# A two-layer mixture-of-experts kernel: sixteen subtractions move from VectorE to GpSimd, and layer 1's dispatch scatters are held to two in flight

## The chip, the cores and the metric

The kernel runs on one core of a Trainium2 chip. The metric is device time in microseconds; a kernel's time is the median of several runs without the profiler. TensorE is called PE, VectorE DVE, ScalarE ACT, GpSimd POOL and SyncE SP, as in the profile.

## The reference

4096 tokens of 128 features (128 sequences of 32) pass through two layers. Each layer first conditions the tokens by a per-sequence table, then sends them through a mixture of experts and a shared expert, and adds the result to the residual.

```python
# layer 0: one expert of 16 for each token
h      = x @ weights[subject] + b[subject]
logits = h @ w_router.T
e      = argmax(logits)
y      = (up * silu(gate)) @ down_proj[e],   gate, up = split((sigmoid(logits[e]) * h) @ gate_up_proj[e])
x      = x + y + shared(h)
# layer 1: two experts of 8 for each token, at most CAP tokens for an expert
h      = layernorm(x + adapter[language](x)) * gamma + beta
first, second = top2(softmax(h @ router_w))
x      = x + g1 * expert[first](h) + g2 * expert[second](h) + 0.1 * shared(h)
```

## The kernel before

There are 32 tiles of 128 tokens (`NT`), taken in 8 groups of four (`NG`, `G`). The program is written out engine by engine; each engine runs its own list in order, and semaphores join them.

**Layer 0, front.** For each group PE transposes the tokens (L1304), multiplies by the subject's weights (L1361), makes router logits (L1380) and transposes the features back into rows. ACT copies those rows into `disp` (L643). DVE picks the expert of each token and, once for every eight tiles (a round, `RT`), computes the row of the expert-sorted buffer that each token goes to (`page_slots`, ends at L918). There are four rounds. GpSimd then scatters the eight tiles of the round into `rows0` in DRAM, one indirect DMA of 128 rows for each tile (L571). Meanwhile ACT, group by group, rounds the 16 experts' gate/up weights to the PE's fp32r format: `w_guh <- w_raw` (L643, `split_rounds`), and counts them on `g_hi`. What the rounding leaves is the low half, `w_gul = w_raw - w_guh`. The two buffers `w_raw` and `w_gul` share their memory, so the subtraction is made in place.

**Layer 0, shared expert.** Once the front is through, PE runs the shared expert of six groups (L1393 up, L1402 down), DVE the product (`glu0`, L958) and the addition to the residual (`add0`, L964). Between these DVE makes the low half, one expert at a time, four experts behind each of the additions 0 to 3 (`low_half`, L978), counted on `g_lo`.

**Layer 0, experts.** PE waits for the six groups, the block table, all 16 low halves (`g_lo`) and the down weights, then goes through 48 blocks of 128 sorted rows: transpose, gate/up in three products (L1426 to L1428), down (L1441). SP loads each block (L450); it starts with the first four as soon as all 32 scatters have landed (`sc0`). DVE writes a block's result (L1015), and GpSimd scatters it back to token order (L582).

**Layer 1.** GpSimd adds the experts' result to the residual of six groups (L376). PE, ACT and DVE run the adapter, the layer norm (L1113 and on) and the router over the 8 groups, in a software pipeline. First choices get their slots in six rounds of 8, 8, 4, 4, 4 and 4 tiles (L1072), second choices all at once at the end (L1177). GpSimd scatters tile by tile, 32 for the first choice and 32 for the second, into `rows1` (L605). Twice among them it adds -T to half of the tokens' codes in `disp` (L612), after a wait until the first-choice scatters of that half have landed. Beside the second-choice scatters PE runs the shared expert, group by group (L1517 to L1519 up, L1603 down). When all 64 scatters have landed, SP loads the first three expert groups (L487). Their transposes (`q_tr(0)`) stand on PE just ahead of the last shared down product, and 40 expert groups follow (L1633 to L1635, L1645).

Of the kernel before, what the change touches and what calls it, by code (L numbers as in the profile page):

```python
# [5 lines left out]
def adaln_moe_two_layers(  # L6
# [29 lines left out]
    fp32 = mybir.dt.float32  # L36
# [5 lines left out]
    ALU = mybir.AluOpType  # L42
# [8 lines left out]
    S = T // B  # L51
    NSUB = c0_w.shape[0]
    E0, _, F0x2 = f0_gate_up.shape
    F0 = F0x2 // 2
    C0 = F0 // P
    NLANG = c1_b2.shape[0]
    A = c1_w1.shape[1] // NLANG
    E1, _, F1 = f1_w1.shape
    C1 = F1 // P
    TOP_K = 2  # L60
# [7 lines left out]
    NT = T // P  # L68
# [42 lines left out]
    with ctx:  # L111
# [3 lines left out]
        def sem(name):  # L115
            return ctx.enter_context(nc.semaphore(name))
# [6 lines left out]
        with ExitStack() as layer0:  # L123
            def sb0(name, shape, dt=fp32):
                return layer0.enter_context(nc.sbuf_tensor(name, shape, dt))
# [3 lines left out]
            w_guh = sb0("w_guh", [P, E0 * F0x2], fp32r)  # L129
            with nc.sbuf_tensor("w_raw", [P, E0 * F0x2], fp32) as w_raw:  # L130
                pass
            w_gul = sb0("w_gul", [P, E0 * F0x2], fp32r)
# [129 lines left out]
        g_hi = sem("g_hi")  # L262
        g_lo = sem("g_lo")
# [75 lines left out]
        sc1 = [[sem(f"sc1_{k}{h}") for h in range(2)] for k in range(2)]  # L339
# [190 lines left out]
        def _(pool):  # L530
            gp = nc.gpsimd
# [29 lines left out]
            gp.tensor_copy(disp[:, :, H:H + 1], codes[:, :].unsqueeze(2)).then_inc(codes0, 1)  # L561


            pool.wait_ge(zero0, 16 * (NBLKP // 4))
            pool.wait_ge(codes0, 1)
            for t in range(NT):
                if t % RT == 0:
                    pool.wait_ge(slots0, t // RT + 1)
                    pool.wait_ge(scored, t // RT + 1)
                    pool.wait_ge(tok_done, (t + RT) // G)  # L570
                gp.indirect_dma_start(rows0, bass.IndirectOffsetOnAxis(ap=slot[:, 0, t:t + 1], axis=0),  # L571
                                      disp[:, t, :], None, bounds_check=NBLKP * P - 1,
                                      oob_is_err=False).then_inc(sc0[t // G % 2], 16)


            last_token = pool.to_reg(T - 1)
            with pool.Fori(0, NBLKP // 8) as it:
                for c in range(8):
# [5 lines left out]
                                          oob_is_err=False).then_inc(by_st[s], 16)  # L584
# [11 lines left out]
            HT = NT // 2  # L596
            for k in range(TOP_K):
                for t in range(NT):
                    if k == 0 and t in first_tiles:
                        r = first_tiles.index(t)  # L600
                        pool.wait_ge(slots1, r + 1)
                        pool.wait_ge(b_tk, (t + round_tiles[r]) // G)
                    if k == 1 and t == 0:
                        pool.wait_ge(slots1, NR1 + 1)
                    gp.indirect_dma_start(rows1, bass.IndirectOffsetOnAxis(ap=slot[:, k, t:t + 1], axis=0),  # L605
                                          disp[:, t, :], None, bounds_check=E1 * CAP - 1,
                                          oob_is_err=False).then_inc(sc1[k][t // HT], 16)
                    if (k, t) in ((0, NT - 8), (1, HT - 8)):
                        h = k
                        pool.wait_ge(sc1[0][h], 16 * HT)  # L610
                        half = slice(h * HT, (h + 1) * HT)
                        gp.tensor_scalar(disp[:, half, H:H + 1], codes[:, half].unsqueeze(2), float(-T), None,  # L612
                                         ALU.add).then_inc(codes1, 1)
                        pool.wait_ge(codes1, h + 1)
# [210 lines left out]
        def _(dve):  # L825
            v = nc.vector
# [125 lines left out]
            def glu0(n):  # L952
                for c in range(C0):
                    dve.wait_ge(sil_done, C0 * n + c + 1)
                    dve.wait_ge(pe_gu, 2 * C0 * n + 2 * c + 2)
                    if n >= 2:
                        dve.wait_ge(pe_dn, n - 1)
                    v.tensor_tensor(act[n % 2][:, c, :], PS[2 * c + 1][:, :], sil[:, c, :],  # L958
                                    ALU.mult).then_inc(act_done, 1)

            def add0(n):
                dve.wait_ge(pe_dn, n + 1)
                a = acc[:, n * G:(n + 1) * G, :]
                v.tensor_tensor(a, a, PS[4][:, :].rearrange("p (i h) -> p i h", h=H), ALU.add).then_inc(acc0, 1)  # L964
# [7 lines left out]
                                        op0=ALU.is_le, op1=ALU.mult))  # L972
            v.tensor_reduce(bexpF[:, :], rank[:, 0:NR * E0], AX.X, ALU.add).then_inc(bx_rows, 1)

            def low_half(e):
                cols = slice(e * F0x2, (e + 1) * F0x2)
                dve.wait_ge(g_hi, e + 1)
                v.tensor_tensor(w_gul[:, cols], w_raw[:, cols], w_guh[:, cols].bitcast(fp32),  # L978
                                ALU.subtract).then_inc(g_lo, 1)

            for n in range(1, NG - NLATE + 1):
                if n < NG - NLATE:
                    glu0(n)
                add0(n - 1)
                for e in range(4 * n - 4, min(4 * n, E0)):
                    low_half(e)
                if n == 2:

                    dve.wait_ge(pe_bx, 1)
                    v.tensor_scalar(w_at[:, 0:NBLKP, 0], PS[6][0:1, 0:NBLKP], float(F0x2), None, ALU.mult)  # L990
                    v.tensor_scalar(w_at[:, 2:NBLKP + 2, 1], PS[6][0:1, 0:NBLKP], float(C0 * H), None,
                                    ALU.mult).then_inc(blocks0, 1)
# [104 lines left out]
            for n in range(NG + 3):  # L1097
# [8 lines left out]
                if 1 <= n < NG + 1:  # L1106
                    m = n - 1
                    k = m % 2
# [179 lines left out]
            for g in range(NG):  # L1288
# [4 lines left out]
                else:  # L1293
                    for i in range(G):
                        t = g * G + i
# [6 lines left out]
        def _(pe):  # L1302
# [33 lines left out]
            for n in range(NG + 1):  # L1336
# [11 lines left out]
                if n < NG:  # L1348
                    pe.wait_ge(xT_done, n + 1)
                    if n == 0:  # L1350
                        pe.wait_ge(ld_c0w, 16)
                        pe.wait_ge(off_ready, 1)
                    _, offs = nc.values_load_multi_w_load_instructions(
                        w0off[0:1, n * GB:(n + 1) * GB], engines=(mybir.EngineType.PE,), min_val=0,
                        max_val=(NSUB - 1) * H, skip_runtime_bounds_check_because="subjects are under NSUB")
                    for b in range(QB):
                        if b == 1 and n >= 3 and n % 2 == 1:
                            rank0((n - 3) // 2)
                        for i in range(G):
                            t = i * QB + b  # L1360
                            last = mm(PS[1 + b][0:S, i * H:(i + 1) * H],  # L1361
                                      xT[n % 2][:, t * S:(t + 1) * S], c0w[:, ds(offs[t], H)],
                                      start=True, stop=True)
                        last.then_inc(pe_c, 1)
# [91 lines left out]
            pe.wait_ge(blocks0, 1)  # L1456
            pe.wait_ge(slots0, NR)
            pe.wait_ge(tok_done, NG)
            pe.wait_ge(g_lo, E0)
            pe.wait_ge(ld_dn, 16)  # L1460

            def pe_stages(j0, turn, offs_g, offs_d):
# [66 lines left out]
            for n in range(NG + 3):  # L1529
# [9 lines left out]
                if n < NG:  # L1539
# [3 lines left out]
                    for c in range(NCH):  # L1543
                        cols = slice(c * P, (c + 1) * P)
# [3 lines left out]
                    for c in range(NCH):  # L1548
                        cols = slice(c * P, (c + 1) * P)
# [178 lines left out]
```

## Time and profile before

| | us |
|---|---|
| median of 3 runs without the profiler | 514.65 |
| lowest and highest of them | 514.14, 516.04 |
| span of the profiled execution, first to last instruction | 571.1 |

The page gives no time of its own for the profiled execution beside its span. That span is 56.45 us longer than the median. Busy shares of the span: PE 81%, DVE 46%, ACT 45%, GpSimd 42%. The page names for each group of instructions how long its engine sat idle before it and what released it; "remote" there, and "another core or an unknown queue" in the chain, stand for a release that the profile could not tie to any instruction.

### The profile page before, as it was taken

Reading aid. Unit: us, or ns where it says so; the run is one execution under the profiler, and the core shown is the slowest. Engines: PE = TensorE matmul, PEld = TensorE weight load, DVE = VectorE, ACT = ScalarE, POOL = GpSimd, SP = SyncE. Lnnn points to the kernel's source line nnn. Section 1 sums busy time; section 2 is a strip of 40 time slices with the busy share of each in tenths; the row PEclk is TensorE's granted clock in tenths of the full one; section 3 lists DMA queues with packets and bytes.
Section 4 is the critical chain, followed back from the end, with each engine's and each line's share of the span. In section 5 each row is a group of like instructions: output and inputs, shape, how many; then the busy total and the mean of one; then the engine's idle time right before and its main releaser. Section 6 shows DMA issues by size and latency. Waiting matters only on the chain.

```text
span 571.1 us, 10130 instructions
## 1 busy us (share of the span) xinstructions
PE 463.1 (81%) x3132; PEld 392.7 (69%) x3133; DVE 261.9 (46%) x831; ACT 255.9 (45%) x596; POOL 238.0 (42%) x255
## 2 busy tenths in 40 slices
PE   6897698978888889999846765489999999999910
PEld 3785564566676766787744655178999999999900
DVE  1144267845555554347447912053433333233475
ACT  2453453235555543556314241034455555555653
POOL 2023535214554555003272777600155555556550
PEclk8997879999999999999787796579999999999975
DMA  9999921102222107400010111110223434313569
GB/s 242 365 340 368 367 66 37 39 23 67 74 71 63 47 11 235 143 2 20 19 51 15 48 48 55 42 47 1 61 76 96 134 107 113 105 50 88 165 182 282
DMA packets 70930, 62.33 MB, mean 109 GB/s; under 512 B 9676, under 2 KB 57439, under 8 KB 70898
## 3 DMA queue, kind: packets, MB, share of 16 engines
q1 hardware_dynamic: 63202, 48.32, 28.5%
q0 software_dynamic: 7168, 12.56, 6.7%
q10 hardware_dynamic: 528, 1.05, 0.6%
q8 instruction: 17, 0.28, 0.2%
q14 instruction: 15, 0.12, 0.1%
HBM read 32.44 MB, written 31.69 MB: 112 GB/s over the span
## 4 chain that ended last, share of the span: by engine, by line
PE 63%; another core or an unknown queue 10%; DVE 9%; DMA 7%; issue 6%; ACT 2%; POOL 1%; SPq 0%; DVEq 0%; POOLq 0%; ACTq 0%
PE PS L1645 11%; PE PS L1304 8%; PE PS L1361 6%; PE PS L1603 5%; PE PS L1441 3%; PE PS L1635 3%; PE PS L1565 3%; PE PS L1633 3%; PE PS L1634 3%; PE PS L1393 2%; PE PS L1402 2%; DMA back1b<-grp_y,grp_i 2%; PE PS L1426 2%; PE PS L1428 1%
## 5 line engine op out<-in xcount | busy, mean ns | idle before, releaser
L623 POOL DMA_INDIRECT back<-grp_y,grp_i x70 | 69.8, 997 | 93.9 <-DVE grp_y L1236 71.0
L605 POOL DMA_INDIRECT rows<-disp,slot x64 | 63.6, 994 | 76.1 <-DVE slot L1072 56.0
L1645 PE MATMUL PS<-w2r,act 128*128 128x128 f32 x640 | 78.1, 275 | 0.5 <-ACT act L789 0.5
L1645 PEld LDWEIGHTS PS<-w2r,act 128*128 128x128 f32 x640 | 74.8, 192 | 0.9 <-DVE grp_y L1236 0.7
L582 POOL DMA_INDIRECT back<-act,blk_i x48 | 46.9, 977 | 60.8 <-DVE act L1015 41.1
L789 ACT ACTIVATE act<-PS,b1r 128x256 f32<-128x256 f32 x160 | 63.7, 477 | 16.5 <-PE PS L1635 14.2
L571 POOL DMA_INDIRECT rows<-disp,slot x32 | 32.6, 1018 | 67.4 <-issue 53.8
L1236 DVE TENSOR_TENSOR grp_y<-PS,b2r 128x256 f32<-128x256 f32 x40 | 17.0, 424 | 89.6 <-PE PS L1645 69.5
L1603 PE MATMUL PS<-sw,act 128*128 128x128 f32 x256 | 37.5, 313 | 14.1 <-issue 11.8
L1633 PE MATMUL PS<-xh,w1h 128*128 128x256 f32 x160 | 48.3, 302 | 0.0
L740 ACT ACTIVATE act<-PS,sb 128x512 f32<-128x512 f32 x32 | 21.4, 688 | 59.6 <-remote 32.9
L1603 PEld LDWEIGHTS PS<-sw,act 128*128 128x128 f32 x256 | 36.5, 228 | 15.4 <-issue 13.5
L1635 PE MATMUL PS<-xh,w1l 128*128 128x256 f32 x160 | 45.2, 283 | 0.0
L643 ACT ACTIVATE xh<-PS 128x256 fp32r<-128x256 f32 (+1 forms) x48 | 20.1, 419 | 55.9 <-PE PS L1304 48.2
L1634 PE MATMUL PS<-xl,w1h 128*128 128x256 f32 x160 | 44.9, 281 | 0.0
L1361 PE MATMUL PS<-c0w,xT 128*32 x256 | 38.7, 321 | 7.4 <-issue 7.4
L1361 PEld LDWEIGHTS PS<-c0w,xT 128*32 128x32 f32 x256 | 32.5, 131 | 12.4 <-issue 9.3
L1441 PEld LDWEIGHTS PS<-w_dn,act 128*128 128x128 f32 x192 | 25.8, 190 | 15.5 <-issue 14.7
L1441 PE MATMUL PS<-w_dn,act 128*128 x192 | 30.9, 283 | 5.5 <-ACT act L643 5.2
L1008 DVE SCALAR_TENSOR_TENSOR act<-PS,blk_x,act 128x256 f32<-128x256 f32 x48 | 23.2, 483 | 20.2 <-ACT act L697 15.7
L643 ACT ACTIVATE t<-PS 32x512 f32<-32x512 f32 x32 | 18.7, 584 | 29.0 <-PE PS L1361 20.7
L1148 DVE SCALAR_TENSOR_TENSOR acc<-PS,acc 128x512 f32<-128x512 f32 x8 | 5.5, 690 | 54.9 <-remote 38.5
(256 smaller groups left out, 1009.9 us busy)
## 6 DMA issues: line engine op xcount, KB each, us to landing
rows<-zrow SPq DMA_DIRECT2D x32, 260.0 KB, 5.0
grp_x<-rows SPq DMA_DIRECT2D x40, 130.0 KB
w_raw<-in_f_gate_up SPq DMA_DIRECT2D x8, 512.0 KB, 10.1
back<-zrow SPq DMA_DIRECT2D x8, 512.0 KB
back<-back SPq DMA_DIRECT2D x16, 256.0 KB, 5.0
blk_x<-rows SPq DMA_DIRECT2D x48, 65.0 KB
acc<-in_x SPq DMA_DIRECT2D x8, 256.0 KB, 5.8
y0g<-back SPq DMA_DIRECT2D x8, 256.0 KB, 3.2
```

What stands on the lines that cost most here:

```text
L582: gp.indirect_dma_start(back0, bass.IndirectOffsetOnAxis(ap=blk_i[c][:, 0:1], axis=0), blk_y[s][:, :], None, bounds_check=last_token, oob_ ...
L605: gp.indirect_dma_start(rows1, bass.IndirectOffsetOnAxis(ap=slot[:, k, t:t + 1], axis=0), disp[:, t, :], None, bounds_check=E1 * CAP - 1, ...
L623: gp.indirect_dma_start(back, bass.IndirectOffsetOnAxis(ap=grp_i[v % NX][:, u:u + 1], axis=0), grp_y[k][:, u, :], None, bounds_check=last, ...
L789: sc.activation(act[k][:, c, 0:UP], PS[1 + k * (C1 // 2) + c // 2][:, (c % 2) * UP:(c % 2 + 1) * UP], ACT.Silu, bias=b1r[e][:, c:c + 1]).t ...
L1304: return nc.tensor.transpose(dst, src, ident[0:k, 0:k])
L1361: last = mm(PS[1 + b][0:S, i * H:(i + 1) * H], xT[n % 2][:, t * S:(t + 1) * S], c0w[:, ds(offs[t], H)], start=True, stop=True)
L1441: last = mm(PS[4 if k == 0 else 7][:, 0:H], blk_aT[k][:, c * P:(c + 1) * P], w_dn[:, ds(off + c * H, H)], start=c == 0, stop=c == C0 - 1)
L1603: last = mm(tile(PS[4], i), tile(act[k][:, c, :], i), sw2[:, c, :], start=c == 0, stop=c == C1 - 1)
L1633: mm(y, high, xh[k][:, 0:UP], start=True, stop=False)
L1634: mm(y, high, xl[k][:, 0:UP], start=False, stop=False)
L1635: last = mm(y, low, xh[k][:, 0:UP], start=False, stop=True)
L1645: last = mm(PS[5 + k][:, u * P:(u + 1) * P], act[k][:, c, u * P:(u + 1) * P], w2r[e][:, c, :], start=c == 0, stop=c == C1 - 1)
```

## The change

Three edits.

1. DVE no longer makes the low halves. GpSimd makes them, half an expert (128x256) behind each of the 32 layer-0 scatters; the half of tile t waits for ACT's rounding of expert t // 2. `g_lo` now counts 32 halves, and PE waits for all of them.
2. In layer 1 each scatter from the third on waits until the one two places before it has landed. The scatters' semaphores now alternate by tile, two for each choice.
3. The wait ahead of each of the two code updates is left out, since edit 2 covers it.

```diff
--- before.py
+++ after.py
@@ -561,6 +561,13 @@
             gp.tensor_copy(disp[:, :, H:H + 1], codes[:, :].unsqueeze(2)).then_inc(codes0, 1)
 
 
+            def low_half(h):
+                cols = slice(h * F0, (h + 1) * F0)
+                pool.wait_ge(g_hi, h // 2 + 1)
+                gp.tensor_tensor(w_gul[:, cols], w_raw[:, cols], w_guh[:, cols].bitcast(fp32),
+                                 ALU.subtract).then_inc(g_lo, 1)
+
+            assert E0 * 2 == NT
             pool.wait_ge(zero0, 16 * (NBLKP // 4))
             pool.wait_ge(codes0, 1)
             for t in range(NT):
@@ -571,6 +578,7 @@
                 gp.indirect_dma_start(rows0, bass.IndirectOffsetOnAxis(ap=slot[:, 0, t:t + 1], axis=0),
                                       disp[:, t, :], None, bounds_check=NBLKP * P - 1,
                                       oob_is_err=False).then_inc(sc0[t // G % 2], 16)
+                low_half(t)
 
 
             last_token = pool.to_reg(T - 1)
@@ -602,12 +610,14 @@
                         pool.wait_ge(b_tk, (t + round_tiles[r]) // G)
                     if k == 1 and t == 0:
                         pool.wait_ge(slots1, NR1 + 1)
+                    n = k * NT + t
+                    if n >= 2:
+                        pool.wait_ge(sc1[(n - 2) // NT][t % 2], 16 * ((n - 2) % NT // 2 + 1))
                     gp.indirect_dma_start(rows1, bass.IndirectOffsetOnAxis(ap=slot[:, k, t:t + 1], axis=0),
                                           disp[:, t, :], None, bounds_check=E1 * CAP - 1,
-                                          oob_is_err=False).then_inc(sc1[k][t // HT], 16)
+                                          oob_is_err=False).then_inc(sc1[k][t % 2], 16)
                     if (k, t) in ((0, NT - 8), (1, HT - 8)):
                         h = k
-                        pool.wait_ge(sc1[0][h], 16 * HT)
                         half = slice(h * HT, (h + 1) * HT)
                         gp.tensor_scalar(disp[:, half, H:H + 1], codes[:, half].unsqueeze(2), float(-T), None,
                                          ALU.add).then_inc(codes1, 1)
@@ -972,18 +982,10 @@
                                         op0=ALU.is_le, op1=ALU.mult))
             v.tensor_reduce(bexpF[:, :], rank[:, 0:NR * E0], AX.X, ALU.add).then_inc(bx_rows, 1)
 
-            def low_half(e):
-                cols = slice(e * F0x2, (e + 1) * F0x2)
-                dve.wait_ge(g_hi, e + 1)
-                v.tensor_tensor(w_gul[:, cols], w_raw[:, cols], w_guh[:, cols].bitcast(fp32),
-                                ALU.subtract).then_inc(g_lo, 1)
-
             for n in range(1, NG - NLATE + 1):
                 if n < NG - NLATE:
                     glu0(n)
                 add0(n - 1)
-                for e in range(4 * n - 4, min(4 * n, E0)):
-                    low_half(e)
                 if n == 2:
 
                     dve.wait_ge(pe_bx, 1)
@@ -1456,7 +1458,7 @@
             pe.wait_ge(blocks0, 1)
             pe.wait_ge(slots0, NR)
             pe.wait_ge(tok_done, NG)
-            pe.wait_ge(g_lo, E0)
+            pe.wait_ge(g_lo, 2 * E0)
             pe.wait_ge(ld_dn, 16)
 
             def pe_stages(j0, turn, offs_g, offs_d):
```

GpSimd's list at the start of the layer-0 scatters, before; the first row stands ahead of them, the DMA rows are the scatters of `disp` to `rows0`:

```order
L561 COPY disp<-codes 128x32 [waits poolk]
L571 DMA rows<-disp,slot 6144x130 [waits scored,slots0,tok_done,codes0,zero0]
L571 DMA rows<-disp,slot 6144x130 x7
L571 DMA rows<-disp,slot 6144x130 [waits tok_done,scored,slots0]
L571 DMA rows<-disp,slot 6144x130 x7
```

and after:

```order
L561 COPY disp<-codes 128x32 [waits poolk]
L578 DMA rows<-disp,slot 6144x130 [waits scored,slots0,tok_done,codes0,zero0]
L567 TENSOR_TENSOR w_gul<-w_raw,w_guh 128x256 [waits g_hi]
L578 DMA rows<-disp,slot 6144x130
L567 TENSOR_TENSOR w_gul<-w_raw,w_guh 128x256 [waits g_hi]
```

The 32 scatters stood one behind the other, with a wait at the start of each round alone; now a subtraction stands between each two, and it waits for `g_hi`.

DVE's list in the shared expert of layer 0, before (L958 is the product, L964 the addition, L978 the low half):

```order
L964 TENSOR_TENSOR acc<-acc,PS 128x512 [waits pe_dn]
L978 TENSOR_TENSOR w_gul<-w_raw,w_guh 128x512 [waits g_hi] x4
L958 TENSOR_TENSOR act<-PS,sil 128x512 [waits pe_dn,pe_gu,sil_done] x2
L964 TENSOR_TENSOR acc<-acc,PS 128x512 [waits pe_dn]
L978 TENSOR_TENSOR w_gul<-w_raw,w_guh 128x512 [waits g_hi] x4
L990 TENSOR_SCALAR w_at<-PS 1x48 [waits pe_bx]
L991 TENSOR_SCALAR w_at<-PS 1x48
L958 TENSOR_TENSOR act<-PS,sil 128x512 [waits pe_dn,pe_gu,sil_done] x2
L964 TENSOR_TENSOR acc<-acc,PS 128x512 [waits pe_dn]
L978 TENSOR_TENSOR w_gul<-w_raw,w_guh 128x512 [waits g_hi] x4
L958 TENSOR_TENSOR act<-PS,sil 128x512 [waits pe_dn,pe_gu,sil_done] x2
```

and after (L968 and L974 are the product and the addition):

```order
L974 TENSOR_TENSOR acc<-acc,PS 128x512 [waits pe_dn]
L968 TENSOR_TENSOR act<-PS,sil 128x512 [waits pe_dn,pe_gu,sil_done] x2
L974 TENSOR_TENSOR acc<-acc,PS 128x512 [waits pe_dn]
L992 TENSOR_SCALAR w_at<-PS 1x48 [waits pe_bx]
L993 TENSOR_SCALAR w_at<-PS 1x48
L968 TENSOR_TENSOR act<-PS,sil 128x512 [waits pe_dn,pe_gu,sil_done] x2
L974 TENSOR_TENSOR acc<-acc,PS 128x512 [waits pe_dn]
L968 TENSOR_TENSOR act<-PS,sil 128x512 [waits pe_dn,pe_gu,sil_done] x2
L974 TENSOR_TENSOR acc<-acc,PS 128x512 [waits pe_dn]
```

The runs of four low halves are gone, and nothing has come in their place.

GpSimd's list where the second-choice scatters of layer 1 begin, before (L612 is the code update):

```order
L605 DMA rows<-disp,slot 10240x130 [waits b_tk,slots1]
L612 TENSOR_SCALAR disp<-codes 128x16 [waits sc1_00]
L605 DMA rows<-disp,slot 10240x130 [waits codes1]
L605 DMA rows<-disp,slot 10240x130 x2
L605 DMA rows<-disp,slot 10240x130 [waits b_tk,slots1]
L605 DMA rows<-disp,slot 10240x130 x3
L605 DMA rows<-disp,slot 10240x130 [waits slots1]
L605 DMA rows<-disp,slot 10240x130 x8
L612 TENSOR_SCALAR disp<-codes 128x16 [waits sc1_01]
L605 DMA rows<-disp,slot 10240x130 [waits codes1]
```

and after (L616 and L622 are the scatter and the update):

```order
L616 DMA rows<-disp,slot 10240x130 [waits sc1_01]
L616 DMA rows<-disp,slot 10240x130 [waits sc1_00,slots1]
L616 DMA rows<-disp,slot 10240x130 [waits sc1_01]
L616 DMA rows<-disp,slot 10240x130 [waits sc1_10]
L616 DMA rows<-disp,slot 10240x130 [waits sc1_11]
L616 DMA rows<-disp,slot 10240x130 [waits sc1_10]
L616 DMA rows<-disp,slot 10240x130 [waits sc1_11]
L616 DMA rows<-disp,slot 10240x130 [waits sc1_10]
L616 DMA rows<-disp,slot 10240x130 [waits sc1_11]
L616 DMA rows<-disp,slot 10240x130 [waits sc1_10]
L622 TENSOR_SCALAR disp<-codes 128x16
L616 DMA rows<-disp,slot 10240x130 [waits sc1_11,codes1]
```

A scatter that followed the last one without a wait now waits on the semaphore of the scatter two before it; the update's own wait is gone.

## Rows read from the trace of the kernel before

**Rows 1.** The page: its head, and the chain that ended last, by engine.

```profile
span 571.1 us, 10130 instructions
PE 63%; another core or an unknown queue 10%; DVE 9%; DMA 7%; issue 6%; ACT 2%; POOL 1%; SPq 0%; DVEq 0%; POOLq 0%; ACTq 0%
```

**Rows 2.** DVE's waits: instruction <- releaser: us, times, longest.

```profile
DVE acc L1148 <- remote: 38.5, 2, 26.1
DVE lg L946 <- remote: 19.1, 2, 10.5
```

**Rows 3.** Layer 1, two stretches: length, busy (count) PE PEld DVE ACT POOL; clock; DMA.

```profile
346.00:373.00 27.00, 12.80 (x39) 8.99 (x38) 0.87 (x4) 2.12 (x4) 17.69 (x18) 0.56 0.18 55
382.76:389.14 6.38, 6.38 (x46) 5.83 (x46) 2.41 (x4) 2.75 (x5) 0.00 (x0) 1.00 0.00 0
```

**Rows 4.** The chain through layer 0's front: start us, us, what.

```profile
30.30 1.00 PE PS L1380 x8
...
37.27 0.99 PE PS L1380 x8
...
43.23 0.99 PE PS L1380 x8
...
78.29 1.00 PE PS L1380 x8
```

**Rows 5.** The chain in layer 1, before the second choice.

```profile
270.29 6.41 another core or an unknown queue
...
293.04 7.50 another core or an unknown queue
```

**Rows 6.** Layer 1 in order of time, all engines: start us, us, instruction [idle before].

```profile
327.23 1.08 POOL L605 DMA_INDIRECT rows<-disp,slot  x1 [0.81 <-issue]
...
330.51 3.73 PE L1603 MATMUL PS<-sw,act 128*128 128x128 f32 x32
...
366.86 0.98 POOL L605 DMA_INDIRECT rows<-disp,slot  x1 [0.30 <-issue]
...
368.15 0.98 POOL L605 DMA_INDIRECT rows<-disp,slot  x1 [0.30 <-issue]
...
370.50 2.43 SPq L487 DMA_DIRECT2D grp_x<-rows  x5
```

**Rows 7.** The chain at layer 0's experts, and at layer 1's last shared product.

```profile
94.37 3.70 PE PS L1393 x8
...
119.56 0.34 PE PS L1304
...
122.83 1.82 DMA blk_x<-rows
...
211.68 2.08 DMA back<-act,blk_i
...
400.69 3.81 PE PS L1603 x32
```

**Rows 8.** The low halves, by tile: ns min/median/max, first and last start us.

```profile
L978 DVE TENSOR_TENSOR w_gul<-w_raw,w_guh x16: 681/683/685, 95.4 to 113.1; 128x512 fp32r<-128x512 f32 x16
```

**Rows 9.** GpSimd in order of time: its first and last scatter of layer 0.

```profile
38.86 1.18 POOL L571 DMA_INDIRECT rows<-disp,slot  x1 [33.99 <-issue]
...
103.39 1.50 POOL L571 DMA_INDIRECT rows<-disp,slot  x1 [0.30 <-issue]
```

**Rows 10.** GpSimd in order of time: its arithmetic, and a scatter ahead of some.

```profile
220.38 6.21 POOL L376 TENSOR_TENSOR acc<-acc,y0g 128x512 f32<-128x512 f32 x5 [7.73 <-DVE acc L376]
...
337.63 0.98 POOL L605 DMA_INDIRECT rows<-disp,slot  x1 [0.30 <-issue]
338.68 0.27 POOL L612 TENSOR_SCALAR disp<-codes 128x16 f32<-128x16 f32 x1
```

**Rows 11.** All engines: a release by DVE, and the scatter that waited for it.

```profile
126.69 0.28 DVE L1015 COPY act<-PS 128x128 f32<-128x128 f32 x1
...
127.79 0.98 POOL L582 DMA_INDIRECT back<-act,blk_i  x1 [0.81 <-issue]
```

## The prediction

> **What bounds the kernel now.** I read the page's chain first: PE holds 63% of the span, and 10% goes to releases that the profile could tie to nothing [rows 1]. That share is 56 us, and the profiled span, 571.1 us, is 56.45 us longer than the median of 514.65. DVE's waits show where they sit: behind no instruction, ahead of the shared additions of layer 1 and the router copies of layer 0 [rows 2]. In those stretches GpSimd issues scatters back to back. From 346 to 373 us PE runs 39 matmuls in 27 us; later the same code runs 46 in 6.38 us at full clock [rows 3].
>
> Are these stalls there without the profiler? I count them by the work. In layer 0 router products follow one another after 6.97 and 5.96 us by turns [rows 4]; the last two rows there span three groups, 43.23 to 78.29, 35.1 us where 19.9 are due: 15.2 us lost. In layer 1 the chain holds 6.41 and 7.50 us more [rows 5]. In the shared expert of layer 1 the down product of group 1 starts at 330.51 [rows 6]; at 6.38 us a group [rows 3] that of group 6 would start at 362.4 and end 3.6 us later, at 366.0. Without stalls PE would then ask for the first expert group. The scatters take longer: the last starts at 368.15, SP issues the load at 370.50 [rows 6], and at the 1.82 us of such a load [rows 7] it is there at 372.3. The last shared down product, 3.8 us, follows and would end at 376.5 with the transpose ahead of it; in the profile it ended at 404.5 [rows 7]. That is 28 us. Together 15.2 + 13.9 + 28 = 57 us, against 56.45 wanted. So I take the stalls as the profiled execution's own, and do my sums in a timeline without them, which I set equal to the median.
>
> In that timeline two things matter. **Layer 0:** PE is fed back to back through the shared expert from 94.37 to the first block's transpose at 119.56 [rows 7]; less 15.2 that is 104.4. **Layer 1:** PE would be ready for the experts at 366.0 and gets its first group at 372.3 (both on the profile's axis behind the last stall), so GpSimd's chain of scatters sets the end there, by 6 us.
>
> **Edit 1, DVE's side.** Sixteen subtractions of 683 ns go [rows 8], 10.9 us of DVE, between 95.4 and 113.8. PE is fed back to back then, so I cost the gain at nothing; if DVE held PE up there, at most a product of 0.7 us would come earlier.
>
> **Edit 1, GpSimd's side.** Its price is not in the trace. Five two-input operations on 512 columns take 6.21 us in a row, 1.24 each, and one on 16 columns 0.27 [rows 10]; a line through both gives 0.74 for 256, and I take 0.72 since two inputs cost no less at the small end. The subtraction starts 0.06 after the scatter's end, as L612 does (338.68 after 337.63 + 0.98) [rows 10]. Behind it I take the 0.30 that separates scatters [rows 10]: 0.98 + 0.06 + 0.72 + 0.30 = 2.06 us a tile, for 1.285 now. At best the last gap is 0.06 too: 1.82. At worst it is a full wake of 0.8 (next part): 2.55. A round of eight then takes 16.5 us, and rounds come 13 us apart (6.97 + 5.96), so GpSimd never catches up: from its first scatter at 38.86 [rows 9] the last starts at 38.86 + 31 × 2.06 = 102.7. Now it starts at 103.39 - 15.2 = 88.2 [rows 9], far ahead of PE. Landing and SP take 2.35 (368.15 to 370.50 [rows 6]), the load 1.82: the first block is there at 106.9. The last low half ends at 104.5, before it. PE wants the block at 104.4. **+2.5 us**; at best 0 (99.5), at worst 38.86 + 31 × 2.55 + 4.2 = 122.1, +17.7. ACT's roundings come a group or more ahead of their use and do not add.
>
> **Edit 2.** Which wait ends last for scatter n? The engine is free 1.285 after n-1, so 2.57 after n-2 started. The landing of n-2: SP acts on one 2.35 us after its start [rows 6], and the chain has 2.08 for one [rows 7]; I take 2.2. A wait that ends late costs a wake: DVE ends at 126.97 and the waiting scatter starts at 127.79, though the engine was free at 126.98: 0.8 us [rows 11]. I find no pair closer than 0.79 in this loop. So scatter n starts 2.2 + 0.79 = 2.99 us after n-2, not 2.57: no more are in flight than before, but each pair costs 0.42 us more (0.30 with a landing of 2.08, 0.57 with 2.35; 0 if the wake runs beside the scatter ahead). The second choice has 32 scatters, 15.5 pairs, one of them already held by the code update: +6.1 us. The first-choice scatters finish late too. The last 24 of them lose 12 × 0.42 = 5 us; the pauses between their rounds give back an estimated 3.5 (0 to 5), so the second choice, which now starts right when its slots are out (0.81 idle [rows 6]), begins about 1.5 later. Queued behind the waiting scatters are only more scatters; SP waits for the last. **+7.5 us** (6.1 + 1.5, rounded), all on the path, since GpSimd's chain was already the later. Bounds 0 and 10.5.
>
> **Edit 3.** Both waits had long been met: the update starts 0.07 us after its scatter [rows 10]. Nothing.
>
> Sum: 514.65 + 2.5 + 7.5 = **524.7 us**.
>
> **A rule against edit 1.** DVE's subtraction has both inputs in SBUF; the last scatter, issued while a run of them was on DVE, takes 1.50 us [rows 9] in place of 0.98 [rows 6], so the two engines may get in each other's way by up to half a microsecond. What would it do here? Most of DVE's slot arithmetic in the front has two SBUF inputs. If each of GpSimd's halves met 0.52 us of it, a tile would take 2.58: 38.86 + 31 × 2.58 + 4.2 = 123.0, +18.6 us in place of +2.5. The Trainium skill, SBUF — State Buffer, section Who interferes with whom,, says that a DVE instruction with two SBUF inputs and a GpSimd one that reads SBUF exclude each other for the whole instruction. By that rule, the row agrees in kind; DVE's slot arithmetic is made of shorter operations than the low half and fills only a part of each round, so I leave it out of the sum and make it a rival.
>
> **The rivals.**
>
> *Nothing happens.* At most two scatters were in flight already (landing 2.2, third issue 2.57), so the cap does nothing if a wait that is met while the scatter ahead is running costs no wake; and a tile at 1.82 keeps layer 0 hidden. For it: waits met early leave the 0.30 gap alone. Against: rows 11, and the landing comes only 0.37 us before the slot. Time 514.7, up to 517.
>
> *Faster.* The stalls are in plain runs too, in part, and come from scatters issued back to back: my count of them has an error of some 10 us, and such a part could hide in the median. Then the slower pace (1.5 for 1.285) lets PE and DVE run on during the second choice, and PE, not GpSimd, was the later there. Were 10 of the 28 us of that stretch in plain runs and gone now, the kernel would take 514.65 - 10 + 2.5 = 507. It decides from a point where stalls in plain runs exceed the 6 us by which GpSimd is later. Against: the count closes without them.
>
> *Much slower.* GpSimd's halves cost 2.55 us a tile or more, by the wake or by DVE: layer 0 +18, with +7.5: 540. It decides from 2.0 us a tile on, at 1 us for each 0.03.
>
> **How the numbers follow.** A measurement of this kernel tells about 0.5% from no change, 2.6 us. Forecast (both costs, 518 to 530) 0.47; nothing 0.18; faster 0.17; much slower 0.18. The predicted time is the forecast's. The range has to hold 0.8: all of the forecast and of nothing, part of faster down to 510, part of much slower up to 536. Faster by over 0.5%: 0.17; within: 0.18; slower: 0.65. The forecast's own range is 518 to 530.
>
> **What the profile after would show.** GpSimd's two-input rows of 256 columns at about 0.72 us, and layer-0 scatters 2.06 us apart in an unbroken row; DVE without low halves, PE no faster in the shared expert; the first block load behind PE's last shared product, and PE waiting there. In layer 1 pairs of scatters 2.99 us apart, with idle time of some 0.5 us ahead of each second one, released by a DMA; the stalls may shrink or grow in the profile, without meaning for the plain time. I am wrong if tiles stand 1.285 us apart in layer 1 still, if PE's first block does not wait for a scatter, or if plain time falls while the scatters slow down.

## The result, and the profile after

The changed kernel takes 544.1 us (541.71, 542.17, 546.24, 546.02), the kernel before 514.76 beside it: ratio 1.0556, interval 1.0499 to 1.0613, so 29 us slower. I had 524.7, and 536 as the upper end. The direction was right, the size was off by a factor of three.

The page of the kernel after, head and chain, against [rows 1]:

```profile
span 540.0 us, 10149 instructions
PE 64%; DMA 11%; issue 10%; DVE 6%; POOL 6%; ACT 1%; SPq 0%; POOLq 0%; DVEq 0%; ACTq 0%
```

Nothing is left of "another core or an unknown queue". DMA has 11% of the chain where it had 7%, GpSimd 6% where it had 1%. The profiled execution took 541.71 us, so here span and time belong together, which was not so in [rows 1].

Because the first trace of before has 57 us of stalls in it, I profiled the kernel before once more (the run is told below); differences "against the second trace" mean that one. It took 520.66 us, at the top of the runs of before, where the trace of after is at the bottom of its own, so the two traces differ by 21.5 us of span where the medians differ by 29. In that trace DMA has 6% of the chain and GpSimd 5%: GpSimd stood on it before the change as well.

**Layer 0.** GpSimd after, in order of time, against [rows 9] and [rows 10]:

```profile
86.31 1.00 POOL L578 DMA_INDIRECT rows<-disp,slot  x1 [0.16 <-issue]
87.33 0.74 POOL L567 TENSOR_TENSOR w_gul<-w_raw,w_guh 128x256 fp32r<-128x256 f32 x1
88.24 0.99 POOL L578 DMA_INDIRECT rows<-disp,slot  x1 [0.17 <-issue]
89.26 0.79 POOL L567 TENSOR_TENSOR w_gul<-w_raw,w_guh 128x256 fp32r<-128x256 f32 x1
92.59 0.99 POOL L578 DMA_INDIRECT rows<-disp,slot  x1 [2.55 <-DVE slot L928]
...
106.06 0.99 POOL L578 DMA_INDIRECT rows<-disp,slot  x1 [0.17 <-issue]
```

A half takes 0.74 us (forecast 0.72) and a tile 1.93 (88.24 - 86.31; forecast 2.06). But the row of scatters is not unbroken: at the last round GpSimd waits 2.55 us for DVE's slots. The last scatter starts at 106.06, and PE, after:

```profile
117.08 2.02 PE L1404 MATMUL PS<-shd,act 128*128 128x128 f32 x16 [0.87 <-DVE acc L974]
119.88 0.33 PE L1306 MATMUL PS<-ident,blk_x 128*128 128x128 f32 x1 [0.78 <-DVE acc L974]
```

PE does not wait for the block, whose scatters are 13.8 us old by then. It arrives late by itself: 119.88, against 111.66 in the second trace of before. So 8.2 us are lost by the end of layer 0's shared expert, and not by GpSimd's list. About half are lost ahead of it and half in it: its first product starts at 74.29 in the second trace of before and at 78.30 after.

```profile
74.29 1.02 PE L1393 MATMUL PS<-featT,shg 128*128 128x512 f32 x2
```

```profile
78.30 1.06 PE L1395 MATMUL PS<-featT,shg 128*128 128x512 f32 x1
```

DVE after, in the slot arithmetic of round 4:

```profile
85.53 0.66 DVE L910 TENSOR_SCALAR padI<-padI 128x16 int32<-128x16 int32 x1
...
86.64 0.79 DVE L917 TENSOR_TENSOR_SCAN t<-ones_f,t 128x16 f32<-128x16 f32 x1
87.47 0.65 DVE L918 TENSOR_SCALAR padF<-t,endE 128x16 f32<-128x16 f32 x1
...
88.57 0.90 DVE L922 TENSOR_TENSOR t<-t 128x128 f32<-128x128 f32 x1
89.50 0.69 DVE L923 TENSOR_TENSOR t<-t 128x128 f32<-128x128 f32 x1
90.23 0.29 DVE L924 TENSOR_TENSOR t<-t 128x128 f32<-128x128 f32 x1
```

L922 to L924 are the same operation on the same shape, 0.29 us when nothing is in the way; beside GpSimd's halves two of the three take 0.69 and 0.90.

**Layer 1.** GpSimd after, at its last scatters, and then PE:

```profile
359.76 0.98 POOL L616 DMA_INDIRECT rows<-disp,slot  x1 [0.46 <-issue]
361.59 0.98 POOL L616 DMA_INDIRECT rows<-disp,slot  x1 [0.85 <-issue]
362.88 0.99 POOL L616 DMA_INDIRECT rows<-disp,slot  x1 [0.30 <-issue]
364.66 0.98 POOL L616 DMA_INDIRECT rows<-disp,slot  x1 [0.80 <-DMA rows<-disp,slot]
```

```profile
344.00 3.73 PE L1605 MATMUL PS<-sw,act 128*128 128x128 f32 x32
369.37 0.66 PE L1306 MATMUL PS<-ident,grp_x 128*128 128x128 f32 x2 [21.63 <-DMA grp_x<-rows]
```

A pair is 3.07 us here (364.66 - 361.59; forecast 2.99); over the whole second choice it is 3.18 (49.26 us for 31 steps). PE stands 21.63 us in front of the first expert group. The parts, in us, from the start of one row to that of the next:

| | second trace of before | after | |
|---|---|---|---|
| start to layer 0's first block transpose | 111.66 | 119.88 | +8.2 |
| to layer 1's first scatter | 138.07 | 138.66 | +0.6 |
| first scatter to first of the second choice | 51.75 | 56.86 | +5.1 |
| first to last scatter of the second choice | 41.08 | 49.26 | +8.2 |
| last scatter to first group's transpose | 4.70 | 4.71 | 0 |
| to the end | 171.2 | 170.6 | -0.6 |

The execution in the left column was a long one, so its differences are small ones. Five other traces here have the front of before; in them the first block comes at 108.5 to 111.4. The nine other traces without a cap of two have 49.1 to 51.7 us for the first choice and 40.8 to 42.1 for the second.

Layer 0 cost 2.5 us in the forecast, the first choice 1.5, the second 6.1. The theory to test: both edits cost, edit 1 by a meeting of GpSimd's and DVE's work, edit 2 by its wakes. Its rivals were that GpSimd's longer list is what costs in layer 0, and that the edits cost only together.

### The profile page after: what moved, and what is told of

It reads as the page before. It is cut to its first block, busy times and chain, and to the rows that moved or that the text cites. A ratio compares the mean times of both kernels' runs of the same rounds, so it can differ in the third digit from the quotient of the medians.

```text
span 540.0 us, 10149 instructions
## 1 busy us (share of the span) xinstructions
PE 449.3 (83%) x3132; PEld 386.2 (72%) x3133; DVE 261.9 (49%) x815; ACT 257.9 (48%) x596; POOL 262.7 (49%) x287
## 4 chain that ended last, share of the span: by engine, by line
PE 64%; DMA 11%; issue 10%; DVE 6%; POOL 6%; ACT 1%; SPq 0%; POOLq 0%; DVEq 0%; ACTq 0%
PE PS L1647 12%; PE PS L1306 8%; PE PS L1363 5%; DMA rows<-disp,slot 5%; PE PS L1395 5%; POOL rows L616 5%; PE PS L1443 4%; PE PS L1567 3%; PE PS L1637 3%; PE PS L1635 3%; PE PS L1636 3%; DMA back1b<-grp_y,grp_i 3%; PE PS L1428 2%; PE PS L1404 2%; PE PS L1430 2%
## 5 line engine op out<-in xcount | busy, mean ns | idle before, releaser
L616 POOL DMA_INDIRECT rows<-disp,slot x64 | 65.0, 1015 | 78.1 <-DVE slot L1074 40.5
L578 POOL DMA_INDIRECT rows<-disp,slot x32 | 32.0, 1000 | 46.1 <-issue 40.7
L1363 PE MATMUL PS<-c0w,xT 128*32 x256 | 33.3, 292 | 7.8 <-issue 7.8
L1363 PEld LDWEIGHTS PS<-c0w,xT 128*32 128x32 f32 x256 | 29.2, 118 | 11.0 <-issue 9.5
L750 ACT ACTIVATE act<-PS,sb 128x512 f32<-128x512 f32 x32 | 21.7, 689 | 25.9 <-PE PS L1521 25.6
L1306 PE MATMUL PS<-ident,grp_x 128*128 128x128 f32 x80 | 15.6, 277 | 21.9 <-DMA grp_x<-rows 21.6
L1605 PEld LDWEIGHTS PS<-sw,act 128*128 128x128 f32 x256 | 33.1, 210 | 0.5
L1605 PE MATMUL PS<-sw,act 128*128 128x128 f32 x256 | 33.3, 293 | 0.0
L1636 PEld LDWEIGHTS PS<-xl,w1h 128*128 128x128 f32 x160 | 30.6, 191 | 0.0
```

Source lines behind the costliest of these rows:

```text
L1306: return nc.tensor.transpose(dst, src, ident[0:k, 0:k])
L1363: last = mm(PS[1 + b][0:S, i * H:(i + 1) * H], xT[n % 2][:, t * S:(t + 1) * S], c0w[:, ds(offs[t], H)], start=True, stop=True)
L1605: last = mm(tile(PS[4], i), tile(act[k][:, c, :], i), sw2[:, c, :], start=c == 0, stop=c == C1 - 1)
L1636: mm(y, high, xl[k][:, 0:UP], start=False, stop=False)
```

## The experiments

### The kernel before, profiled again

> The kernel before, unchanged, profiled once more. If the stalls of its first trace (about 57 us) belong to that one execution, this span is 512 to 518 us, the first block's transpose starts at 108.5 to 111.5 and the first expert group's of layer 1 at 345 to 346 on this trace's axis, with no release that the profile can't tie to an instruction. If they come with every profiled execution of it, the span is near 571 us again.

Time 514.77 against 516.35 (ratio 0.9993, 0.9938 to 1.0048). Span 518.5 us, without an untied release. PE in this trace:

```profile
111.66 0.33 PE L1304 MATMUL PS<-ident,blk_x 128*128 128x128 f32 x1 [0.78 <-DVE acc L964]
...
347.26 0.66 PE L1304 MATMUL PS<-ident,grp_x 128*128 128x128 f32 x2 [4.09 <-DMA grp_x<-rows]
```

The 57 us belonged to that one execution, as the prediction took it. PE waits 4.09 us for the first group: GpSimd's chain sets the end there, as forecast (by 6). Block and group came 0.2 and 1.3 us later than the upper ends I gave, and the span is 0.5 over, in an execution that was itself long.

### Each edit alone

Of the diff's five pieces, edit 1 alone is the first, second, fourth and fifth; edits 2 and 3 alone are the third.

> Edit 1 alone. Theory A (both edits cost, about equally): layer 0's experts start some 15 us late because GpSimd's subtractions, which read SBUF, hold up the slot arithmetic of DVE; +13 to +16 us, about 529, with DVE's operations in the front stretched by up to 0.6 us and GpSimd idle at the start of rounds behind DVE. Theory B (GpSimd's own list is the late one): +2 to +4 us, about 517.5, DVE's operations as before. Theory C (the two edits cost only together): within 2 us of before.

> Edits 2 and 3 alone. Theory A: pairs of scatters 3.0 to 3.1 us apart in both choices, so +13 to +16 us, about 529. Theory B (the price predicted, with the first choice absorbed by pauses): +7.5 us, 522. Theory C: within 2 us of before.

Edit 1: 526.26 us, ratio 1.0169 (1.0103 to 1.0235), +9 us. Edits 2 and 3: 533.43, ratio 1.031 (1.0243 to 1.0376), +16 us. Together 25, where both at once cost 29 with an interval of 26 to 32: that they cost only together is out, and within the intervals they add. The equal halves of 13 to 16 that I expected were a miss for edit 1. The chain of edit 1's trace shows how the time gets onto the path:

```profile
77.45 5.82 PE PS L1393 x8
...
84.52 0.58 DVE padI L907
...
85.54 0.79 DVE t L911
...
86.36 0.68 DVE t L915
...
87.58 0.67 DVE t L919
...
88.27 0.79 DVE t L920
...
91.55 0.69 DVE act L966
...
92.28 5.40 PE PS L1393 x8
```

PE's next up product (L1393) needs the buffers that DVE's product (L966) reads, and that product stands on DVE behind the slot arithmetic of round 4. So PE waits for slots, though it uses none of them. The row of round 3 stands on the chain in the same way, from 65 to 74 us, ahead of the last router product; in the second trace of before no slot arithmetic is on the chain between 58 and 80 us. From the pick of the expert on, the four rounds have 96 operations of slot arithmetic. In the second trace of before 1 of them is longer by over 0.05 us than the shortest of its line in the traces with the front of before, by 0.3 us; with edit 1 alone 26, by 11.3 us in all, and after 25, by 10.2. The last slots come 14.25 us after the last scores here (76.56 to 90.81), 10.98 in the second trace of before.

GpSimd in the trace of edits 2 and 3 alone:

```profile
308.27 1.08 POOL L608 DMA_INDIRECT rows<-disp,slot  x1 [0.82 <-DMA rows<-disp,slot]
309.66 0.98 POOL L608 DMA_INDIRECT rows<-disp,slot  x1 [0.30 <-issue]
311.45 0.97 POOL L608 DMA_INDIRECT rows<-disp,slot  x1 [0.81 <-DMA rows<-disp,slot]
```

From the first scatter to the first of the second choice (at 302.96) it takes 56.96 us, to the last of the second choice 50.71 more: +5.2 and +9.6 against the second trace of before. Its PE waits 21.7 us for the first group.

### What of the cap costs: four and three in flight

```diff
-        sc1 = [[sem(f"sc1_{k}{h}") for h in range(2)] for k in range(2)]
+        sc1c = [sem(f"sc1c_{j}") for j in range(4)]
...
+                    if n >= 4:
+                        m = n - 4
+                        pool.wait_ge(sc1c[m % 4], 16 * (m // 4 + 1))
```

The scatters count on the four in turn, SP waits for all, and the waits ahead of the code updates go. The other run has three semaphores in the same way.

> The kernel before with at most four scatters of layer 1 in flight instead of two, update waits left out. If what costs is that the wait for a landing (about 2.2 us) ends after the engine is free, a cap of four never holds (the fourth before started 5.1 us earlier): 514 to 516. If it is the semaphores, or a wait instruction as such ahead of each scatter, that costs: +5 us or more.

> At most three scatters of layer 1 in flight. Theory A (what costs is a landing that comes later than the engine): the third before started 3.86 us earlier and landed at about 2.2 to 2.4, before the engine is free even with a wake of 0.8 (3.0 to 3.2): within 2 us of before. If the wake is charged whatever the landing: +10 us or more.

Four: 516.78 against 517.26, ratio 0.9973 (0.9938 to 1.0009). Three: 518.24 against 516.22, ratio 1.0026 (0.9993 to 1.0058). Two lines of GpSimd's waits, the first with four, the second with three in flight:

```profile
POOL rows L608 <- DMA rows<-disp,slot: 11.9, 39, 0.3
```

```profile
POOL rows L608 <- DMA rows<-disp,slot: 15.3, 47, 0.8
```

Of the 64 scatters 55 wait for no slots and no codes. With four in flight all of these start in the ordinary 0.30 us behind the end of the one ahead: a wait that is met early costs nothing. With three, 2 of the 55 take more than 0.35; with two, 39 do, in the trace of edits 2 and 3 alone. The landings in that trace and in the trace of after show by what rule: a scatter starts 0.79 us after the landing that it waits for, or 0.30 after the end of the scatter ahead, whichever is later. That gives the start within 0.03 us for 103 of 108 scatters. The last scatter after is an example: the one at 361.59, two places ahead of it, lands at 363.88, and the last starts at 364.66. So a wait costs nothing only if its landing comes at least 0.49 us (0.79 - 0.30) before the engine is free. With a landing 2.29 us after the start, a pair takes 3.08 us (2.29 + 0.79). So it is the lateness of the landing, and no semaphore or wait as such, that edit 2 pays for; edit 3 is in all these runs and costs nothing.

### GpSimd reads, GpSimd writes: what holds up DVE

In both runs DVE keeps its low halves, and GpSimd does something useless behind each of the first 31 scatters; the last scatter waits for the last of these operations:

```diff
...
+                if t < NT - 1:
+                    if t >= 1:
+                        pool.wait_ge(fil, t)
+                    gp.tensor_tensor(act1[:, 0:F0], zrow[:, 0:F0], zrow[:, F0:2 * F0], ALU.subtract).then_inc(fil, 1)
```

In the other run the operation is `gp.memset(act1[:, 0:784], 0.0)`.

> The kernel before, DVE keeps its low halves; behind each of the first 31 scatters of layer 0 GpSimd makes a subtraction that nothing needs: two inputs in SBUF, 128x256, about 0.74 us. Theory A (GpSimd's reading operations hold up DVE's slot arithmetic): as much as edit 1 alone, +8 to +10 us, DVE's slot operations stretched. Theory D (edit 1 costs by what depends on the halves, g_lo or the waits for the roundings): within 2 us of before.

> As the run with the useless subtraction, but the filler is a memset of 784 columns, about as long (0.74 us), which reads nothing. Theory A in its narrow form (it is the reading that excludes DVE): scatters spaced as in edit 1 but DVE's operations as before, 0 to +2 us. Theory B (GpSimd's longer list is the cost): +8 to +10 us as with the subtraction.

The subtraction: 529.23, ratio 1.0223 (1.0172 to 1.0275), +11.5 us. So edit 1's price has nothing to do with the halves' data, their count or the roundings. That it is 2.5 us more than edit 1 lies within the two intervals. The memset: 522.79, ratio 1.0112 (1.0082 to 1.0141), +5.8 us: neither of the two numbers I had. Its scatters are as far apart (1.92). DVE beside the memsets:

```profile
81.57 1.53 DVE L909 CAST t<-padI 128x16 f32<-128x16 int32 x1
...
83.34 0.19 DVE L914 TENSOR_TENSOR_SCAN t<-ones_f,t 128x16 f32<-128x16 f32 x1
83.57 1.44 DVE L915 TENSOR_SCALAR padF<-t,endE 128x16 f32<-128x16 f32 x1
...
85.46 0.29 DVE L919 TENSOR_TENSOR t<-t 128x128 f32<-128x128 f32 x1
```

and beside the useless subtractions:

```profile
85.85 0.65 DVE L909 CAST t<-padI 128x16 f32<-128x16 int32 x1
...
86.97 0.76 DVE L915 TENSOR_SCALAR padF<-t,endE 128x16 f32<-128x16 f32 x1
87.77 0.66 DVE L916 TENSOR_TENSOR t<-padF,t 128x16 f32<-128x16 f32 x1
...
89.00 0.77 DVE L920 TENSOR_TENSOR t<-t 128x128 f32<-128x128 f32 x1
```

Beside a GpSimd operation that only writes, eight conversions and operations with a scalar are longer, by 7.6 us in all, and no operation with two inputs is, but for one that only stands behind a long cast. Beside one that reads, both kinds are (25 operations, 11.3 us). The Trainium skill (SBUF — State Buffer, section Who interferes with whom) states just this split: a DVE operation with two SBUF inputs excludes only a GpSimd one that reads, while copy, cast and tensor_scalar in their two-port modes exclude any. The traces agree on both halves. They add a size: a cast of 0.17 us takes up to 1.53, twice the memset's 0.77, and ends within 0.04 us of its end, though it began during the scatter ahead. The profile does not say which of DVE's operations ran in a two-port mode.

```profile
81.33 0.97 POOL L574 DMA_INDIRECT rows<-disp,slot  x1 [0.17 <-issue]
82.28 0.78 POOL L580 MEMSET act<- 128x784 f32 x1
```

### The same pace by waits alone

```diff
+                m = t - 1 if t % RT in (2, 5) else t - 2
+                if m >= 0:
+                    pool.wait_ge(sc0[m % 2], 16 * (m // 2 + 1))
```

The scatters count on two semaphores by turns here, as in layer 1 after the change.

> The kernel before with layer 0's scatters made slow by waits alone: two in flight at most, and twice in each round of eight only one, so a tile takes GpSimd about 1.9 us as in edit 1, but GpSimd touches SBUF no more often than before. Theory A (what costs is GpSimd's and DVE's work meeting in SBUF): 0 to +2 us, DVE's slot operations as before. Theory B (the longer list itself): +5 to +9 us.

532.88, ratio 1.0308 (1.0255 to 1.0361), +16.5 us, and neither theory's number: the pace was not 1.9 us a tile but 2.6. In the front a scatter takes long to land, as the layer-0 scatters of the run with edits 2 and 3 alone have it:

```profile
DMA to landing us min/median/max: 2.3/4.3/7.1
```

GpSimd in the run at hand, a wait of round 1 and its last scatter, and then PE:

```profile
47.58 0.98 POOL L574 DMA_INDIRECT rows<-disp,slot  x1 [5.78 <-DMA rows<-disp,slot]
...
119.46 0.98 POOL L574 DMA_INDIRECT rows<-disp,slot  x1 [0.90 <-DMA rows<-disp,slot]
```

```profile
104.87 2.02 PE L1405 MATMUL PS<-shd,act 128*128 128x128 f32 x16 [0.87 <-DVE acc L967]
123.95 0.45 PE L1307 MATMUL PS<-ident,blk_x 128*128 128x128 f32 x1 [17.05 <-DMA blk_x<-rows]
```

The run is of use all the same. Here GpSimd's list is far longer than in edit 1 (last scatter 119.46, not 105.22), and PE still ends its shared products at 106.9, no later than in the second trace of before, with DVE's slot operations longer by 0.6 us in all. A long list on GpSimd does not slow the front; it costs only where PE comes to wait for the block, 4.49 us behind the last scatter. For edit 1 alone that is 105.22 + 4.49 = 109.7, 9.5 us before PE gets there at 119.2. So the list, rival B, is out.

### The halves behind the last scatter

Edit 1, with the 32 halves moved out of the loop to behind it (`for t in range(NT): low_half(t)`).

> Edit 1, but GpSimd makes all 32 halves behind its last scatter of layer 0. Theory A: DVE's slot arithmetic is as before (it is over by then), so the front keeps its pace; the last half ends about 32 x 0.8 = 26 us behind the last scatter, at 92 to 95 + 1 + 26 = 119 to 122, where PE wants it at 109 to 111: +8 to +12 us by the halves' own chain, with PE waiting in front of its first gate/up product and the scatters spaced 1.285 us. If DVE's relief from the halves is worth something, PE's last shared products come earlier than before.

523.89, ratio 1.0122 (1.0072 to 1.0172), +6.3 us where 8 to 12 were expected. Its GpSimd, and then PE:

```profile
92.82 21.88 POOL L567 TENSOR_TENSOR w_gul<-w_raw,w_guh 128x256 fp32r<-128x256 f32 x32
```

```profile
105.74 2.02 PE L1404 MATMUL PS<-shd,act 128*128 128x128 f32 x16 [0.87 <-DVE acc L974]
115.06 0.45 PE L1306 MATMUL PS<-ident,blk_x 128*128 128x128 f32 x1 [7.29 <-POOL w_gul L567]
```

The slot arithmetic is as before again (0.4 us longer in all). What costs now is the other thing, 21.88 us of halves in front of PE, which waits 7.29; they end at 114.70, not at 119 to 122, at 0.68 a half and not 0.8. And PE's two waits for DVE's addition (0.87 here, 0.87 in the second trace of before) are as they were with the low halves on DVE. From its first product to its last the shared expert takes PE 36.7 us, and 36.4 to 36.6 in the traces of before: relieving DVE is worth nothing. With GpSimd's halves or subtractions in the loop it takes 40.8 to 42.1, with the memsets 40.7.

### An order that is faster: the last shared product first

```diff
             pe.wait_ge(s_sl, C1 * (NG - 1) + 1)
-            q_tr(0, 0)
             shared1_down(NG - 1, (NG - 1) % 2)
+            q_tr(0, 0)
```

> The kernel before with PE's last shared down product of layer 1 placed ahead of the first expert group's transpose. If GpSimd's chain of scatters sets the end of layer 1's shared part (prediction: by 6 us), PE has 3.8 us of work to put into its wait: -3 to -4 us, 511. If PE is the later there, 0 to +1 us.

> The same exchange of two steps in the kernel before, measured more closely: -4 to -5.5 us (first look -4.96), since both PE's work and GpSimd's chain then end at 344.8 to 345.0.

> The changed kernel with PE's last shared down product ahead of the first expert group's transpose. PE waits 21.6 us there for a load that GpSimd's last scatter sets, so the 3.7 us of the product fit into it: -3.5 to -4 us against the changed kernel, ratio to before about 1.048. If PE's order had no part in it: as the changed kernel, 1.056.

Here PE does the product while it would wait for the load. In the kernel before: 512.3 against 517.26, ratio 0.9891 (0.9824 to 0.9957), and in the longer measurement 512.64 against 516.33, ratio 0.9913 (0.988 to 0.9947): -4.5 us. PE in the first of these traces:

```profile
341.25 3.81 PE L1603 MATMUL PS<-sw,act 128*128 128x128 f32 x32 [1.60 <-DVE acc L1150]
344.96 0.44 PE L1304 MATMUL PS<-ident,grp_x 128*128 128x128 f32 x2
```

The wait for the load (4.09 in the second trace of before) is filled with the product. In the changed kernel the same exchange gives ratio 1.0462 (1.0397 to 1.0527) where it was 1.0556: 4.8 us by the ratios, within their intervals of the 3.7 expected. The kernel before with this exchange is the fastest of all runs here; neither edit belongs in it.

## Why the prediction was right and wrong

- **The stalls of the first trace** were that execution's own. Right, and shown by the second trace. Faster by the stalls (507) falls with it.
- **GpSimd's chain sets the end in layer 1**, by 6 us: measured 4.09. Right.
- **Edit 1, DVE's side**, at most a product of 0.7 us earlier: right for what DVE no longer does. The step of the prediction that failed is what it left out of the sum, that the halves act on what stays on DVE. I had the rule and the 1.50 us scatter of [rows 9], and sent them to a rival because "DVE's slot arithmetic is made of shorter operations than the low half and fills only a part of each round". That reads the interference from the wrong side. I asked how much GpSimd would be held up; it hardly was (0.74 to 0.79 a half). The short operations are the ones that pay, 0.2 or 0.3 us long and 0.4 to 0.6 longer when they meet a half, and they stand in one dependent row.
- **Edit 1, GpSimd's side**, +2.5 us: its pieces were close (1.93 for 2.06 a tile), the conclusion wrong. The +2.5 rested on PE asking for the block at 104.4. In the second trace it asks at 111.66, at 108.6 in the trace of edits 2 and 3 alone. My subtraction of the stalls put it 4 to 7 us too early; in no trace with the halves between the scatters was GpSimd the later. That PE's first block waits for no scatter is one of the signs of being wrong that the prediction names. +2.5 forecast, +9 measured, by another mechanism.
- **Edit 2 as a whole**, +7.5: measured +16 alone. The mechanism, a landing that comes too late for the next scatter but one, was right; both of its terms were too small.
- **Edit 2, second choice**, +6.1: measured +9.6 alone and +8.2 in the changed kernel. A steady pair takes 3.07 to 3.08 us, not 2.99, as a landing that releases a scatter comes some 2.3 us after its issue; the mean pair takes 3.27 alone and 3.18 in the changed kernel, as some scatters run longer and land later. The scatters sit idle 9 us beyond their 0.30 in either trace.
- **Edit 2, first choice**, +1.5: measured +5.2 alone and +5.1. I let the last 24 scatters lose 5 us, 0.21 each, and pauses give back 3.5. The pauses did their part: 10 us of them stand in the second trace of before (6.7, 2.5 and 0.8), and they gave back about 5. The loss was the error: some 10 us over all 31, 0.3 each. Single scatters wait up to 2.04 us for a landing, and others 0.5 to 0.7 each, where the alternation of pairs is broken.
- **Edit 3**, nothing: right.
- **The rivals.** "Nothing" is out: a wait met less than 0.49 us before the engine is free does cost. "Much slower" gave 540 and is the nearest in number, by "the wake or DVE"; but it charged GpSimd's list, 2.55 us a tile, and the list stayed at 1.93. Its number came out by luck, its mechanism did not.
- **The range** ended at 536; 544 lies outside it. Two terms had been bounded at +17.7 and +10.5, 28 together, and I cut between them.

Left open: 4 us between the sum of the edits alone (25) and both (29), which the intervals don't separate. The traces leave nothing over that only both edits at once would make: the front of edit 1's trace and the scatters of the other's, put end to end, give 540.5 us (119.16 + 138.04 + 107.67 + 4.77 + 170.87), and the changed kernel's span is 540.0. Open too is why the front of the same code reaches the first block at 108.5 in one trace and at 111.7 in another.

## What to carry to other kernels

Before moving work from DVE to GpSimd, list what runs on DVE at the same time: if it is a dependent row of small operations on SBUF, each may wait for one of GpSimd's, and the row's end, not GpSimd's, is where to look. A limit on transfers in flight is free as long as the awaited landing comes well before the engine is free, 0.49 us here; if it comes later, the next transfer starts 0.79 us after the landing. Here four and three in flight could not be told from no limit, two cost 3%. When a trace is much longer than the runs, profile again before building a timeline by subtraction.

## What the hardware showed unexpectedly

- A scatter holds GpSimd for 0.98 us in both layers, but lands 2.3 to 7.1 us after its issue in layer 0's front and about 2.3 us after it in layer 1, with single ones up to 3.5. In the trace of edits 2 and 3 alone the landings of 4.5 to 7.1 us start before 66 us, while the page has the DMA queues moving 235 to 369 GB/s; the later ones are there in 2.3 to 4.2. A cap of two costs 3% there; one in the front, a little tighter, cost 3% with PE 17 us idle.
- A 16-column cast on DVE took 1.53 us beside a scatter and a memset of GpSimd, nine times its 0.17. It began during the scatter and ended with the memset behind it; the tensor_scalar of 1.44 us (83.57 to 85.01) did the same with the next pair (memset 84.21 to 84.98). The profile shows that much, not why the scatter's end did not let them through.
- GpSimd's halves back to back take 0.68 us, 0.74 behind a scatter, and the gap ahead of the next scatter is 0.17 behind arithmetic where it is 0.30 behind a scatter.
- One profiled execution of the kernel before was 56 us longer than its runs, the second 2 us shorter than its own time, with the same code.
